# A transformer block on one core: ScalarE takes the first fourteen attention units, and VectorE the residual

## The chip, the core and the metric

The kernel is one program on one NeuronCore of a Trainium2 chip. The metric is device time in microseconds (us), from the host's view of one execution; the profile shows one such execution, taken by the hardware profiler, and its span from the first instruction to the last. Engines are named as in the profile: PE is TensorE (matmul; PEld its weight loads), DVE is VectorE, ACT is ScalarE, POOL is GpSimd, SP is SyncE, which only issues DMAs here.

## What is computed

Input x is 8 sequences of 1024 tokens, 128 channels wide. With xn the layer norm of x, the block gives x + attention(xn) + experts(xn):

```python
x = L0_attn_x
xn = _layernorm(x, axis=-1)
x = x + _L0_attn_ref(xn, ...) + _L0_ffn_ref(xn, ...)
# attention: 8 heads, q and k two wide, v sixteen wide; leaky instead of plain scores
scores = jnp.einsum('bmhd,bnhd->bhmn', q, k) / math.sqrt(dqk)
scores = jnp.where(scores >= 0, scores, 0.2 * scores)
beta = jax.nn.softmax(scores, axis=-1)
out = jnp.einsum('bhmn,bnhd->bmhd', beta, v).reshape(B, M, C)
return gamma * out + x
# experts: RMS norm, softmax router over 16 experts, top 2, capacity 1024 rows an expert
pos = jnp.sum(jnp.cumsum(oh, axis=0) * oh, axis=-1) - 1
keep = pos < CAP
...
h = jax.nn.gelu(jnp.einsum('ech,efh->ecf', dm, fc1_weight) + fc1_bias[:, None, :], approximate=False)
out_mlp = jnp.einsum('ecf,ehf->ech', h, fc2_weight) + fc2_bias[:, None, :]
```

Twelve of the sixteen experts are MLPs; one gives zero, one copies, two give constants. Attention returns its own input too, so the residual is x + xn + gamma * attention + experts.

## The kernel before

Tokens lie in 64 tiles of 128 (partitions) x 128 channels: `y` holds x and becomes the output, `xn` the layer norm. The program has these stages.

**Projections** (`groups(prologue)` in every engine): 16 groups of four tiles. A helper runs 22 steps; at step n each engine does the parts of group n, n-1, n-2, ... whose turn it is, so that engines overlap by lags. TensorE transposes and multiplies (L780 q and k, L784 v and router, L801 directions, L774 the scores' bounds), ScalarE copies out of PSUM, VectorE splits and keeps maxima (L984, L988), GpSimd makes remainders (L410, L415), SyncE stores q and k parts to DRAM (`store_parts`). `groups` takes a table `meanwhile`: functions that an engine calls behind given steps.

**Routing** sits behind and inside the last steps. VectorE finds the two best experts (`first_value` ... `second_choice`, lines 1027 to 1048), counts them (L1067), scans (L1072); TensorE turns counts into positions with two matmuls (L809), VectorE reads these from PSUM (L1076, L1080, semaphore `at_rdy`). GpSimd makes indices and weights (lines 590 to 610). ScalarE meanwhile makes the residual in place, `y = (1 + rstd) * y - mean * rstd`, 64 activations at L702. The scratch of the routing lies in `pr`, the buffer that attention's exponentials also use; the exponentials' first buffers are free early, the seventh unit waits for `route`.

**Attention of three sequences** (`attention(0, BH)`), then **twelve experts**, then **attention of the other five**. Attention goes by units: a pass is one sequence, four heads and 512 queries and has 16 units, 64 units a sequence. For unit i, TensorE makes scores into a PSUM ring of three slots (L820, semaphore `s1`), VectorE rectifies them in place (L1112, `relu`), TensorE adds the linear part and the shift (L830, `s2`), ScalarE takes the exponential (L724, `exps`), and TensorE multiplies with the values (L850, `pv`). Behind a pass VectorE transposes the sums (L1088), GpSimd divides (`quotient`, L445), SyncE moves them across partitions (`spread`, L334, 16 DMAs), GpSimd adds them to `y` (L458).

**Scatter.** During the first attention GpSimd sends the rows of xn to their expert slots in DRAM (`disp`) with 128 indirect DMAs (L496), eleven or twelve a pass for eleven passes; it also scales xn by `r2` (L491), a sequence at a time. `paced` makes a scatter wait for a number of exponentials. The quotient of pass p-1 stands in the middle of the scatters of pass p, in GpSimd's program order.

**Experts.** SyncE's queue holds, in this order: the spread of pass 9, a wait for all scatters (`scat`), the loads of expert 0 (weights and rows of `disp`), the spread of pass 10, a wait, the loads of expert 1; then, in a loop, the store of an expert and the loads of the one after next. VectorE's `turn_rows(e)` scales the weights (L1130) and transposes the rows (L1133), `expert_rows(e)` adds the second bias (L1142); TensorE runs L890 and L901, ScalarE the Gelu. GpSimd has a loop of its own beside them: for each of 8 batches of eight tiles eight instructions of 128x1024 (L623, L631, L634, L637) add the copy and constant experts and a bias to `y`, reading `xn`, which they overwrite.

Most waits are written out by hand as semaphore counts: `wait_ge(S["s1"], i + 1)`. An engine runs its program strictly in order, so what stands behind a wait waits too.

Of the kernel before, what the change touches and what calls it, by code (L numbers as in the profile page):

```python
# [12 lines left out]
P = 128  # L13
# [47 lines left out]
TURN = 5  # L61
BLOCK = 32
# [39 lines left out]
def build(nc, x, consts, w_qk, b_qk, w_vr, b_v, r_b, n_w, n_w_row, w1t, b1, w2t, b2, cvec, gamma, out):  # L102
# [4 lines left out]
    with ExitStack() as ctx:  # L107
# [3 lines left out]
        def sem(name):  # L111
# [23 lines left out]
        (mean, var, rstd, r2, s4, s5, s6, s7) = (st[:, k, :] for k in range(8))  # L135
        y_scale, y_bias = s6, s4
# [19 lines left out]
        moved = sb("moved", [P, 2, HG, GT, DV])  # L156
        rowones = sb("rowones", [1, M], BF16)
# [15 lines left out]
        rt = [ef[:, k, :] for k in range(2 * HG)]  # L173
        ex = rt[1]
        rbf = [rt[k // 2].bitcast(BF16)[:, (k % 2) * NT * E:(k % 2 + 1) * NT * E] for k in range(4 * HG)]
        oh1, oh2, rank_of, reset, cnt, incl = rbf[4:10]
        prod = rt[5], rt[6]
        small = rt[7].rearrange("p (k t) -> p k t", t=NT)
# [6 lines left out]
        xt = sb("xt", [P, CAP])  # L185
# [11 lines left out]
        ps_acc = ps[:, 6:8, :]  # L197
# [5 lines left out]
                 "qz_init weighted at_rdy sum_rdy inv_rdy row_step route ones_rdy max_rdy off_rdy reset_rdy r_exp cnt_rdy pos_rdy ztile init_rdy kz_init "  # L203
                 "ld0 ld1 vp_rdy s1 relu s2 exps pv acc_evac o_rdy turned rg_rdy att_rdy spread0 spread1 y_att "
# [33 lines left out]
        CO0 = 2  # L238

# [20 lines left out]
        def _(sp):  # L260
# [35 lines left out]
            groups(store_parts)  # L296
            for u in range(2):
                sp.wait_ge(S[f"parts_out{u}"], 64 * B)
                sp.wait_ge(S[f"shift_out{u}"], 16 * B)
            sp.wait_ge(S["kz_init"], 16 * NHG * HG)  # L300

            def load_operands(b, hg):
# [3 lines left out]
                for g in range(HG):  # L306
# [8 lines left out]
                    sp.dma_start(q2[o:o + 1, hg, :], qrows[NPROD:NROW, :]).then_inc(S[f"ld{hg}"], 16)  # L315

# [27 lines left out]
            for hg in range(NHG):  # L344
                load_operands(0, hg)
# [50 lines left out]
        def _(pool):  # L396
# [23 lines left out]
            pool.wait_ge(S["zero_in"], 16 * E_MLP)  # L420
# [132 lines left out]
            def attention(b0, b1, move):  # L553
                first, last = b0 * NPB, b1 * NPB - 1
                for p in range(first, last + 1):
                    b = p // NPB

                    def results():

                        if p % NPB == 0:  # L560
                            value_rows(b, 1)
# [16 lines left out]
            value_rows(0, 0)  # L578
# [33 lines left out]
            pool.sem_inc(S["route"], 1)  # L612
            pool.wait_ge(S["y_upd"], B)
# [31 lines left out]
        def _(act):  # L645
# [9 lines left out]
            act.activation(r2, s5, ACT.Sqrt).then_inc(S["stat_a"], 1)  # L655
# [37 lines left out]

            def expert_exponentials():
# [12 lines left out]
            expert_exponentials()  # L707
            for b in range(B - 3, B):
                residual(b)
            act.wait_ge(S["at_rdy"], 1)  # L710
# [7 lines left out]
            def exponentials(i):  # L718
# [5 lines left out]
                act.activation(pr[:, c % BUFS, 2 * pair:2 * pair + 2, :], ring[i % RING], ACT.Exp, scale=SLOPE  # L724
                               ).then_inc(S["exps"], 1)

            def attention(b0, b1):
                first, end = b0 * NUB, b1 * NUB
                for i in range(first, end):
                    if i == (BUFS - 1) * PAIRS + 1:  # L730
                        act.wait_ge(S["route"], 1)
# [481 lines left out]
```

## Time and profile before

| what | us |
|---|---|
| median of 3 runs | 930.86 (929.11 to 931.17) |
| the profiled execution | 931.08 |
| its span | 929.3 |

| engine | busy us | share of the span | instructions |
|---|---|---|---|
| PE | 851.2 | 92% | 7403 |
| DVE | 763.9 | 82% | 883 |
| ACT | 676.9 | 73% | 787 |
| POOL | 602.1 | 65% | 610 |

Of the span, the projections end at about 97 us, the routing at about 126, the first attention at about 362, the experts at about 533. The shares are averages over stages with different limits, so they are read stage by stage: in the routing TensorE hardly works, in attention VectorE and TensorE are both near full, in the experts TensorE alone is.

In a row of the timeline stand the start, the length, engine and line, the operation, what it writes and reads with partitions x elements, how many instructions are merged, and in brackets the idle time of the engine before it and what ended that. SPq is SyncE's DMA queue. "issue" is time in which an engine waited for nothing that the profile shows.

### The profile page before, as it was taken

The numbers are of one execution on the slowest core, as the hardware profiler recorded it, in microseconds if no ns is written. First come the engines' busy times: TensorE is split into PE (matmuls) and PEld (weight loads), VectorE is DVE, ScalarE is ACT, GpSimd is POOL, SyncE is SP. The second block draws the span as 40 slices with busy tenths as digits, with TensorE's granted clock in tenths as the row PEclk, the third lists the DMA queues.
The fourth block names the chain that finished last, engine by engine and source line by source line (L and its number), as shares of the span: only waits on it lengthen the run. The fifth ranks groups of instructions, "written<-read, shape, count | busy, mean of one in ns | idle before, by whom it ended". The sixth has DMA issues, their size and how long they took to land.

```text
span 929.3 us, 19960 instructions
## 1 busy us (share of the span) xinstructions
PE 851.2 (92%) x7403; PEld 338.5 (36%) x7404; DVE 763.9 (82%) x883; ACT 676.9 (73%) x787; POOL 602.1 (65%) x610
## 2 busy tenths in 40 slices
PE   0687269999999999999999999999999999999997
PEld 0454112222222224776776722222222222222222
DVE  5798899999999996322321399999999999999996
ACT  0578888888888888344344388888888888888886
POOL 3355247777777662999999426567566675766772
PEclk9999669999999999999999999999999999999999
DMA  8733101111111014355364111012112011200202
GB/s 220 301 68 77 31 28 33 49 40 52 50 25 37 21 30 92 88 137 126 86 141 125 40 48 40 21 28 59 29 30 60 25 35 27 77 23 17 68 16 54
DMA packets 130167, 59.34 MB, mean 64 GB/s; under 512 B 83498, under 2 KB 120194, under 8 KB 130080
## 3 DMA queue, kind: packets, MB, share of 16 engines
q1 hardware_dynamic: 120464, 48.06, 20.3%
q0 software_dynamic: 8192, 9.37, 3.7%
q8 instruction: 54, 0.88, 0.4%
q10 hardware_dynamic: 1424, 0.76, 0.4%
q14 instruction: 33, 0.27, 0.1%
HBM read 31.58 MB, written 30.02 MB: 66 GB/s over the span
## 4 chain that ended last, share of the span: by engine, by line
PE 59%; DVE 25%; issue 8%; ACT 3%; POOL 2%; DMA 1%; SPq 1%; POOLq 0%; DVEq 0%; ACTq 0%
DVE ps L1112 20%; PE ps L850 18%; PE ps L830 11%; PE ps L820 11%; PE ps L901 9%; PE ps L890 9%; DVE ot L1088 2%; PE ps L780 1%; DMA y<-in_x 1%; ACT pr L675 1%; DVE bst L947 1%; ACT pr L724 1%; SPq L262 1%; POOL ot L410 1%; ACT va L684 1%
## 5 line engine op out<-in xcount | busy, mean ns | idle before, releaser
L1112 DVE TENSOR_SCALAR ps<-ps 128x1024 f32<-128x1024 f32 x512 | 600.3, 1224 | 15.1 <-PE ps L820 12.1
L724 ACT ACTIVATE pr<-ps 128x1024 f32<-128x1024 f32 x512 | 524.0, 1024 | 104.6 <-PE ps L830 70.7
L850 PE MATMUL ps<-pr,vp 128*32 128x256 f32 x4096 | 327.7, 392 | 0.3
L830 PE MATMUL ps<-q,kz 64*128 64x512 bf16 x1024 | 200.6, 389 | 10.1 <-DVE ps L1112 4.3
L820 PE MATMUL ps<-q,kz 62*128 62x512 bf16 x1024 | 200.8, 390 | 2.9 <-DMA q<-parts_dram 1.4
L511 POOL DMA_INDIRECT xs<-eout,idxs x128 | 129.1, 1008 | 107.5 <-ACT pr L724 82.3
L496 POOL DMA_INDIRECT disp<-xn,idx x128 | 125.8, 983 | 50.4 <-issue 28.2
L745 ACT ACTIVATE pr<-ps,b1s 128x512 f32<-128x512 f32 x96 | 66.0, 687 | 96.4 <-PE ps L890 96.4
L830 PEld LDWEIGHTS ps<-q,kz 64*128 64x128 bf16 x1024 | 48.9, 92 | 226.1 <-DVE ps L1112 187.7
L850 PEld LDWEIGHTS ps<-pr,vp 128*32 128x32 f32 x4096 | 81.1, 108 | 120.5 <-issue 118.1
L1130 DVE TENSOR_SCALAR w<-w,nw 128x512 f32<-128x512 f32 x12 | 14.1, 1175 | 94.6 <-DMA pr<-disp 50.6
L901 PEld LDWEIGHTS ps<-w,pr 128*128 128x128 f32 x768 | 87.7, 192 | 6.2 <-issue 6.2
L820 PEld LDWEIGHTS ps<-q,kz 62*128 62x128 bf16 x1024 | 49.4, 93 | 106.9 <-ACT pr L724 76.7
L901 PE MATMUL ps<-w,pr 128*128 128x128 f32 x768 | 88.0, 275 | 0.0
L890 PE MATMUL ps<-xt,w 128*128 128x512 f32 x192 | 84.7, 593 | 0.6 <-issue 0.6
L634 POOL TENSOR_TENSOR y<-y,xn x24 | 56.6, 2358 | 4.9 <-POOL xn L631 4.9
L531 POOL TENSOR_TENSOR y<-y,xs 128x256 f32<-128x256 f32 x64 | 46.5, 727 | 11.4 <-POOL y L531 5.7
L458 POOL TENSOR_TENSOR y<-y,moved 128x256 f32<-128x256 f32 x32 | 23.3, 730 | 44.3 <-DMA moved<-att 28.5
L890 PEld LDWEIGHTS ps<-xt,w 128*128 128x128 f32 x192 | 35.5, 190 | 40.9 <-issue 40.9
L410 POOL TENSOR_TENSOR ot<-pr,parts 112x512 f32<-112x512 f32 x16 | 18.9, 1179 | 37.3 <-ACT parts L680 37.2
L524 POOL TENSOR_TENSOR xs<-xs,co 128x256 f32<-128x256 f32 x64 | 37.9, 616 | 0.6
L792 PE MATMUL ps<-cst,xn 128*128 128x128 f32 x64 | 10.5, 291 | 27.5 <-DVE xn L966 27.5
(120 smaller groups left out, 527.4 us busy)
## 6 DMA issues: line engine op xcount, KB each, us to landing
moved<-att SPq DMA_DIRECT2D x480, 8.0 KB
disp<-pr SPq DMA_DIRECT2D x12, 512.0 KB, 4.8
eout<-pr SPq DMA_DIRECT2D x12, 512.0 KB, 3.0
y<-in_x SPq DMA_DIRECT2D x8, 512.0 KB, 7.5
out<-y SPq DMA_DIRECT2D x7, 512.0 KB, 3.4
w<-in_w1t SPq DMA_DIRECT2D x12, 256.0 KB, 3.1
w<-in_w2t SPq DMA_DIRECT2D x12, 256.0 KB, 3.3
xs<-disp SPq DMA_DIRECT2D x24, 128.0 KB, 3.5
```

The source lines that it names most:

```text
L496: pool.indirect_dma_start(out=disp, out_offset=bass.IndirectOffsetOnAxis(ap=idx[:, k, s * TB + t:s * TB + t + 1], axis=0), in_=xn[:, s * T ...
L511: pool.indirect_dma_start(out=g1[:, g % 2, t, c, :], out_offset=None, in_=eout, in_offset=bass.IndirectOffsetOnAxis(ap=idxs[:, c, GB * i + ...
L531: pool.tensor_tensor(yt, yt, rows[:, :, c, :], ALU.add).then_inc(S["comb" if c else "weighted"], 1)
L634: pool.tensor_tensor(yb, yb, xb, ALU.add).then_inc(S["pool_step"], 1)
L724: act.activation(pr[:, c % BUFS, 2 * pair:2 * pair + 2, :], ring[i % RING], ACT.Exp, scale=SLOPE).then_inc(S["exps"], 1)
L745: act.activation(hs[:, f, half * HALF:(half + 1) * HALF], ps[:, 2 + n % 4, :], ACT.Gelu, bias=b1s[:, u, f:f + 1]).then_inc(S["gel"], 1)
L820: last = pe.matmul(ring[i % RING][:, k, :], kz[r:r + ONES, hg, pair, kc * P:(kc + 1) * P], q2[r:r + ONES, hg, qh * HALF:(qh + 1) * HALF], ...
L830: last = pe.matmul(ring[i % RING][:, k, :], kz[r:r + TILE, hg, pair, kc * P:(kc + 1) * P], q2[r:r + TILE, hg, qh * HALF:(qh + 1) * HALF], ...
L850: last = pe.matmul(acc[p % 2][32 * g:32 * g + 32, cols], vp[:, hg, kc, g, :], pr[:, c % BUFS, g % PAIRS * 2 + g // PAIRS, cols], start=(kc ...
L890: pe.matmul(ps[:, 2 + n % 4, :], w1[:, 2 * u * FFN + f * P:2 * u * FFN + (f + 1) * P], xt[:, half * HALF:(half + 1) * HALF], start=True, s ...
L901: mm = pe.matmul(o, hs[:, f, j * P:(j + 1) * P], w1[:, (2 * u + 1) * FFN + f * P:(2 * u + 1) * FFN + (f + 1) * P], start=(f == 0), stop=(f ...
L1112: dve.tensor_scalar(s, s, 0.0, 1.0 / SLOPE - 1.0, ALU.max, ALU.mult).then_inc(S["relu"], 1)
```

## The change

- ScalarE does the first fourteen units alone, while VectorE is still in the routing: it rectifies them (a Relu in place, `relu_a`) and takes their exponentials, in a written-out order behind the last steps of the projections. These units use two slots of the PSUM ring (banks 0 to 3), and the position matmuls move from banks 6 and 7 to banks 4 and 5. TensorE's order is written out likewise: `first_scores`, `second_pair`, `third_pair`, `later_pairs`; the position matmuls stand between the units. VectorE starts with unit 14.
- The table of the exponential is loaded behind step 3 of the projections (`ready(ACT.Exp)`).
- SyncE loads the operands of the first sequence between the stores of the projections, one head behind each of the steps 8 to 15, and not behind all of them.
- The residual leaves ScalarE. VectorE makes it in the experts as `y = y + xn * rms`, 64 instructions (`scalar_tensor_tensor`): eight ahead of expert 1, 32 behind `expert_rows(0)`, 24 behind `expert_rows(1)`. GpSimd's loop waits for `y_upd`, batch by batch; the first attention's sums are then already in `y`. The wait of GpSimd for the whole residual ahead of attention goes, and so does ScalarE's wait for `route`.
- The routing's scratch moves from `pr` to buffers that are free then (`w1`, `xs`, `parts`, `ot`, `xt`). GpSimd copies both halves of the first values ahead of the routing.

```diff
+FIRST = 14
...
-        (mean, var, rstd, r2, s4, s5, s6, s7) = (st[:, k, :] for k in range(8))
-        y_scale, y_bias = s6, s4
+        (mean, var, rstd, r2, s4, s5, s6, rms) = (st[:, k, :] for k in range(8))
...
+        flat = [w1[:, k * NT * E:(k + 1) * NT * E] for k in range(2)]
+        xflat = xs[:].rearrange("p u t c -> p (u t c)")
+        ex = flat[0]
+        oh1, oh2, rank_of, cnt, reset, incl = (
+            half.bitcast(BF16) for v in (flat[1], xflat, pflat) for half in (v[:, 0:NT * E // 2], v[:, NT * E // 2:NT * E]))
+        prod = flat[0], ot[:].rearrange("p a m -> p (a m)")
+        small = xt[:].rearrange("p (k t) -> p k t", t=NT)
...
-        ps_acc = ps[:, 6:8, :]
+        ps_pos = ps[:, 4:6, :]
...
+        def slot(i):
+
+            return ring[i % 2 if i < FIRST else i % RING]
...
+            def first_operands(k):
+
+                if k == 0:
+                    sp.wait_ge(S["kz_init"], 16 * NHG * HG)
+                    for u in range(2):
+                        sp.wait_ge(S[f"parts_out{u}"], 64)
+                        sp.wait_ge(S[f"shift_out{u}"], 16)
+                load_operands(0, k // HG, range(k % HG, k % HG + 1))
+
+            groups(store_parts, {8 + k: lambda k=k: first_operands(k) for k in range(H)})
...
-            pool.wait_ge(S["zero_in"], 16 * E_MLP)
+            pool.wait_ge(S["dir_rdy"], 2 * B)
+            for u in range(2):
+                pool.wait_ge(S[f"parts_out{u}"], 64 * B)
...
-            value_rows(0, 0)
+            for hg in range(NHG):
+                value_rows(0, hg)
...
-            pool.sem_inc(S["route"], 1)
-            pool.wait_ge(S["y_upd"], B)
             attention(0, BH, scatter)
...
                 pool.wait_ge(S["scat"], 16 * GS)
+                pool.wait_ge(S["y_upd"], b + 1)
...
-            def residual(b):
-
-                for t in range(b * TB, (b + 1) * TB):
-                    last = act.activation(y[:, t, :], y[:, t, :], ACT.Identity, scale=y_scale[:, t:t + 1],
-                                          bias=y_bias[:, t:t + 1])
-                last.then_inc(S["y_upd"], 1)
-
-            groups(prologue, {2 * B + 1 + b: lambda b=b: residual(b) for b in range(B - 3)})
...
+            def rectify(i):
+
+                act.wait_ge(S["s1"], i + 1)
+                act.activation(slot(i), slot(i), ACT.Relu, scale=1.0 / SLOPE - 1.0).then_inc(S["relu_a"], 1)
...
+            groups(prologue, {
+                3: lambda: ready(ACT.Exp),
+                2 * B + 1: lambda: first_units(("R", 0), ("R", 1), ("E", 0), ("E", 1), ("R", 2)),
+                2 * B + 2: lambda: first_units(("R", 3), ("E", 2), ("E", 3), ("R", 4), ("R", 5)),
+                2 * B + 3: lambda: first_units(("E", 4), ("E", 5), ("R", 6), ("R", 7)),
+                2 * B + 5: lambda: first_units(("E", 6), ("E", 7), ("R", 8), ("R", 9))})
+            expert_exponentials()
+            for i in range(8, FIRST, PAIRS):
+                first_units(("E", i), ("E", i + 1))
+                if i + PAIRS < FIRST:
+                    first_units(("R", i + 2), ("R", i + 3))
+            attention(0, BH, FIRST)
...
+            def first_pair(j, behind):
+
+                shifted(2 * j)
+                if j > 0:
+                    values(j - 1, 0)
+                behind()
+                shifted(2 * j + 1)
+                if j > 0:
+                    values(j - 1, 1)
...
+            def first_scores():
+
+                pe.wait_ge(S["v_rdy"], 2 * B)
+                pe.wait_ge(S["xnt_rdy"], 2 * B)
+                scores(0)
+                pe.wait_ge(S["v_evac"], 2 * B)
+                pe.wait_ge(S["lg_rdy"], 2 * B)
+                scores(1)
+                first_pair(0, nothing)
+                scores(2)
...
+            def later_pairs():
+
+                scores(7)
+                for j in range(3, FIRST // 2 - 2):
+                    first_pair(j, nothing)
+                    scores(2 * j + 2)
+                    scores(2 * j + 3)
+                positions(0, cbf[:, C_TRI:C_TRI + P], cnt)
+                first_pair(FIRST // 2 - 2, lambda: positions(1, onesb[:], incl))
+                scores(FIRST - 2)
+                scores(FIRST - 1)
+                pe.wait_ge(S["pos_read"], 2)
+                first_pair(FIRST // 2 - 1, lambda: scores(FIRST))
+                scores(FIRST + 1)
+
+            groups(prologue, {2 * B: first_scores, 2 * B + 1: second_pair, 2 * B + 2: third_pair})
+            later_pairs()
+            attention(0, BH, FIRST)
...
+            def residual(first, last):
+
+                for b in range(first, last):
+                    for t in range(b * TB, (b + 1) * TB):
+                        ins = dve.scalar_tensor_tensor(out=y[:, t, :], in0=xn[:, t, :], scalar=rms[:, t:t + 1],
+                                                       in1=y[:, t, :], op0=ALU.mult, op1=ALU.add)
+                    ins.then_inc(S["y_upd"], 1)
+
+            dve.wait_ge(S["y_att"], BH * NPB)
+            residual(0, 1)
+            for u in range(2):
+                turn_rows(u + 1, 1 - u)
+                expert_rows(u, u)
+                residual(1 + 4 * u, 5 + 3 * u)
+            with dve.Fori(1, E_MLP // 2 - 1) as k:
```

## Rows read from the trace of the kernel before

**Rows 1.** The page's chain that ended last, by line, shares of the span.
```profile
DVE ps L1112 20%; PE ps L850 18%; PE ps L830 11%; PE ps L820 11%; PE ps L901 9%; PE ps L890 9%; DVE ot L1088 2%; PE ps L780 1%; DMA y<-in_x 1%; ACT pr L675 1%; DVE bst L947 1%; ACT pr L724 1%; SPq L262 1%; POOL ot L410 1%; ACT va L684 1%
```

**Rows 2.** The chain in order of time, 376:410 us; start, length, what.
```profile
377.22 0.59 issue
...
377.81 7.11 PE ps L890 x16
...
392.06 6.87 PE ps L890 x16
```

**Rows 3.** Timeline of VectorE, routing; start, length, line, operands, count [idle before].
```profile
123.64 2.35 DVE L1080 TENSOR_REDUCE pr<-pr 128x64 f32<-128x1024 f32 x2
...
125.90 3.59 DVE L1112 TENSOR_SCALAR ps<-ps 128x1024 f32<-128x1024 f32 x3
...
134.03 12.03 DVE L1112 TENSOR_SCALAR ps<-ps 128x1024 f32<-128x1024 f32 x10 [0.74 <-PE ps L820]
```

**Rows 4.** Timeline of ScalarE, routing.
```profile
98.27 3.19 ACT L702 ACTIVATE y<-y,st 128x128 f32<-128x128 f32 x8
...
117.15 1.28 ACT L697 ACT_TABLE_LOAD   x1
```

**Rows 5.** Timeline of TensorE, routing.
```profile
102.91 0.61 PE L774 MATMUL ps<-hat,bok 128*32 128x512 bf16 x1
```

**Rows 6.** Stretches: length, busy time (instructions) by engine, granted clock, DMA.
```profile
core 0: us, PE busy (x) PEld busy (x) DVE busy (x) ACT busy (x) POOL busy (x), PEclk, DMA share, GB/s
...
104.00:116.00 12.00, 0.71 (x2) 0.20 (x2) 11.66 (x16) 11.95 (x31) 0.00 (x0) 0.50 0.01 1
...
134.00:140.00 6.00, 5.92 (x64) 1.77 (x68) 5.84 (x5) 4.95 (x6) 4.53 (x9) 1.00 0.00 0
```

**Rows 7.** GpSimd: scatter grouped, 140:337 (count, busy, mean, idle before); its timeline.
```profile
L496 POOL DMA_INDIRECT disp<-xn,idx x122 | 119.8, 982 | 48.7 <-issue 26.5 <-ACT pr L724 20.9 <-POOL xn L491 1.0
...
140.52 1.23 POOL L496 DMA_INDIRECT disp<-xn,idx  x1 [1.15 <-issue]
...
337.01 0.63 POOL L445 TENSOR_TENSOR att<-ot,rg 128x256 f32<-128x256 f32 x1
```

**Rows 8.** Timeline of SyncE's queue at the start of the experts.
```profile
337.67 10.79 SPq L334 DMA_DIRECT2D moved<-att  x16
...
367.32 4.87 SPq L361 DMA_DIRECT2D pr<-disp  x4
```

**Rows 9.** Timeline of VectorE, experts 0 to 2.
```profile
374.15 2.41 DVE L1130 TENSOR_SCALAR w<-w,nw 128x512 f32<-128x512 f32 x1 [8.01 <-DMA pr<-disp]
...
377.64 1.18 DVE L1142 TENSOR_TENSOR pr<-ps,parts 128x1024 f32<-128x1024 f32 x1
...
387.47 1.02 DVE L1130 TENSOR_SCALAR w<-w,nw 128x512 f32<-128x512 f32 x1 [8.65 <-DMA xs<-disp]
...
388.41 1.23 DVE L1133 STREAM_TRANSPOSE xt<-xs 128x1024 f32<-128x1024 f32 x1
```

**Rows 10.** Timeline of GpSimd in its own loop beside the experts.
```profile
369.16 2.35 POOL L623 TENSOR_TENSOR xn<-xn,nwr 128x1024 f32 x1 [0.36 <-POOL co L618]
...
371.78 1.90 POOL L631 TENSOR_TENSOR xn<-xn,co  x1 [0.26 <-POOL xn L623]
...
385.85 2.35 POOL L637 TENSOR_TENSOR y<-y,bvg 128x1024 f32 x1 [0.19 <-POOL y L634]
...
388.16 2.55 POOL L623 TENSOR_TENSOR xn<-xn,nwr 128x1024 f32 x1
```

**Rows 11.** Timeline of VectorE and GpSimd in the projections, two groups.
```profile
48.31 1.11 DVE L966 TENSOR_SCALAR xn<-y,st 128x128 f32<-128x128 f32 x4
...
49.08 1.35 POOL L410 TENSOR_TENSOR ot<-pr,parts 112x512 f32<-112x512 f32 x1 [0.64 <-ACT parts L680]
...
50.11 0.41 DVE L1010 TENSOR_TENSOR lg<-lg,rb 128x64 f32<-128x64 f32 x1
...
97.51 0.22 DVE L1010 TENSOR_TENSOR lg<-lg,rb 128x64 f32<-128x64 f32 x1
```

**Rows 12.** The page's group of GpSimd's L410: busy, mean ns, idle before.
```profile
L410 POOL TENSOR_TENSOR ot<-pr,parts 112x512 f32<-112x512 f32 x16 | 18.9, 1179 | 37.3 <-ACT parts L680 37.2
```

More of the change, by code:

```diff
@@ L238, in build @@
         CO0 = 2
+        def slot(i):
+            return ring[i % 2 if i < FIRST else i % RING]
+        assert FIRST % RING == 2 and FIRST % 2 == 0
         def unit_of(i):
@@ L692, in prologue, with ready @@
                     act.copy(xnt[:, u, :], ps_t).then_inc(S["xnt_rdy"], 1)
+            def ready(function):
+                act.activation(table[:], gam[:], function, scale=0.0)
             def expert_exponentials():
@@ L723, in exponentials, with attention @@
                     wait_done(act, "pv", c - BUFS + 1)
-                act.activation(pr[:, c % BUFS, 2 * pair:2 * pair + 2, :], ring[i % RING], ACT.Exp, scale=SLOPE
+                act.activation(pr[:, c % BUFS, 2 * pair:2 * pair + 2, :], slot(i), ACT.Exp, scale=SLOPE
                                ).then_inc(S["exps"], 1)
-            def attention(b0, b1):
+            def attention(b0, b1, done=0):
                 first, end = b0 * NUB, b1 * NUB
-                for i in range(first, end):
-                    if i == (BUFS - 1) * PAIRS + 1:
-                        act.wait_ge(S["route"], 1)
+                for i in range(first + done, end):
                     if i == BH * NUB:
@@ L802, in prologue @@
                     last.then_inc(S["dir_rdy"], 1)
-            groups(prologue)
-            for n, (lhs, rhs) in enumerate(((cbf[:, C_TRI:C_TRI + P], cnt), (onesb[:], incl))):
-                pe.wait_ge(S["cnt_rdy"], n + 1)
-                for half in range(2):
-                    last = pe.matmul(ps_acc[:, half, :], lhs, rhs[:, half * HALF:(half + 1) * HALF], start=(n == 0),
-                                     stop=(n == 1))
-            last.then_inc(S["pos_rdy"], 1)
             def scores(i):
@@ L867, in ahead, with attention @@
                     scores(i)
-            def attention(b0, b1):
+            def attention(b0, b1, done=0):
                 first, end = b0 * NUB, b1 * NUB
-                for i in range(first, end):
+                for i in range(first + done, end):
                     shifted(i)
@@ L904, in expert, with positions, nothing, second_pair @@
                 mm.then_inc(S["fc2"], 1)
-            ahead(0, AHEAD)
-            attention(0, BH)
+            def positions(n, lhs, rhs):
+                pe.wait_ge(S["cnt_rdy"], n + 1)
+                for half in range(2):
+                    last = pe.matmul(ps_pos[:, half, :], lhs, rhs[:, half * HALF:(half + 1) * HALF], start=(n == 0),
+                                     stop=(n == 1))
+                if n == 1:
+                    last.then_inc(S["pos_rdy"], 1)
+            def first_pair(j, behind):
[6 more added lines that the diff above has]
+                    values(j - 1, 1)
+            def nothing():
+                pass
+            def first_scores():
[7 more added lines that the diff above has]
+                scores(2)
+            def second_pair():
+                scores(3)
+                first_pair(1, nothing)
+                scores(4)
+                scores(5)
+            def third_pair():
+                first_pair(2, nothing)
+                scores(6)
+            def later_pairs():
[14 more added lines that the diff above has]
+            attention(0, BH, FIRST)
             for u in range(2):
```

85 lines of the change are left out of this document (39 added, 46 removed).

## The prediction

> **What bounds the kernel now.** I read the chain of waits first. By line it is VectorE's rectifying pass (L1112), then TensorE's lines of attention and experts [rows 1]; so VectorE sets the pace in attention and TensorE in the experts. Its stretch at the expert start then shows where one begins to bind: TensorE stands 0.59 us before expert 1 at 377.81 and is gapless from there, expert 2 at 392.06 [rows 2]. Then I read the routing, engine by engine. VectorE ends the position sums at 123.64 + 2.35 = 125.99, begins unit 0 at 125.90 and is steady from 134.03, unit 6: ten units in 12.03 [rows 3]. ScalarE is free of the projections from 98.27 and spends the time on the residual [rows 4].
>
> GpSimd needs a look of its own. It gets the positions at 125.99, issues its first scatter at 140.52, 14.5 later, and comes to the ninth pass's quotient at 337.01 [rows 7]. SyncE stores that result from 337.67 and only behind it, in its queue, loads the experts' rows: those of expert 1 from 367.32, for 4.87 [rows 8]. VectorE idles 8.01 for just that load at 374.15 [rows 9]. So expert 1 does not hang on the end of attention; it hangs on GpSimd's scatter, 40.1 us behind 337.67.
>
> **Part by part: the first units.** Fourteen units taken off VectorE are 14 x 1.2 = 17 us [rows 3]. They need ScalarE twice each. A pass of ScalarE over 128x1024 is not in my rows; VectorE takes 1.2 for the same shape, an upper end, and I take 1.03 for ScalarE, so 28 passes are 29 us from 98.27, to about 130 with TensorE's answers between them. VectorE's own routing work keeps its length but now waits in three places. (1) The next to last hat (L988) waits for a small matmul (L774) that TensorE now issues behind the scores of units 0 to 2, so behind three ScalarE passes: 98.27 + 3.1 = 101.4, then a score and L774, near 102.2. Before, L774 had run long ago, and VectorE came there at about 100.7: 1.5 to 1.7. (2) The last hat waits for the L774 behind unit 5's scores. ScalarE does two more passes, then needs the matmuls behind hat (1), near 104 to 104.7, then four more passes: 108 to 108.8, with score and L774 near 108.6 to 109.6. VectorE is there six us behind (1), near 108: 0.5 to 1.7. (3) The second position matmul now stands in TensorE's queue behind ScalarE's first pass of unit 10: twelve passes and some small ones behind (2), near 123 to 123.8; its sums come at 124 to 126, VectorE's scan ends near 122 to 123.5, 1.1 of this gap was there before: 0.6 to 1.6. Low ends hold with TensorE at the higher of its two levels, high ends at the lower; it sits at 0.50 through 104 to 116 and L774 takes 0.61 there [rows 5, 6]. Sum 2.6 to 5.0; I take 3.7. Positions at 129.7, VectorE's unit 14 there and not at about 143.6 (134.03 + 8 x 1.2): attention ends 11 to 12 us sooner.
>
> GpSimd's scatter starts 3.7 later, though. From there it runs at its own pace more than before. Of 48.7 us of idle before its 122 issues, 122 x 0.30 and 8 x 0.67 (behind a scaling) come with each issue; 6.7 are waits [rows 7]. With attention 12 sooner and the scatter 3.7 later these go. Bounds 4 to 6.7, I take 5; a value copy moved ahead adds 0.5. The Exp table load moves from 117.15 into group 3 of the projections; it takes 1.28 [rows 4], and ScalarE's pause there covers part: 0 to 1.3, I take 0.7. The twelve load issues per half that SyncE now makes between its stores fall into its pauses; nothing. The arithmetic on the mean and two tiny VectorE ops that go: nothing. So expert 1's data come at -0.7 (that is 0.7 + 3.7 - 5.5, or -1.1), bounds -5 to +3; I take -1. **The 12 us of attention are thus mostly not kept**: they end as TensorE idling before the experts.
>
> **The residual.** ScalarE's residual [rows 4] was under the routing, on an engine with nothing better to do. Now VectorE does it in the experts: 64 tiles, eight ahead of expert 1's weights, 32 between the results of expert 0 and the weights of expert 2 (turn_rows(2)), 24 before those of expert 3. By length it fits: four 128x128 tiles took 1.11 [rows 11], 0.26 apart, so 32 are 8.3, and VectorE idled 8.65 before 387.47 [rows 9].
>
> But each tile reads two SBUF tensors (xn and y), and GpSimd is at that time in its own loop over SBUF, 1.90 to 2.55 long instructions with 0.26 or less between them, none at a batch's edge (385.85 + 2.35 = 388.20 against 388.16), 19.0 a batch [rows 10]. What happens to such an op is shown by one pair of rows. L1010 (lg + rb, both SBUF) takes 0.22 at 97.51. At 50.11 it meets GpSimd's L410, in flight from 49.08 to 50.43, and takes 0.41: it ends at 50.52, 0.09 behind GpSimd [rows 11]. It was held until GpSimd's instruction ended. L1130, another form, is held alike: at 374.15 it takes 2.41 under an instruction that ran to 376.3, at 387.47 only 1.02 [rows 9]. The Trainium skill, "SBUF — State Buffer", section "Who interferes with whom", states this for two SBUF inputs against a GpSimd instruction that reads SBUF: whichever started first keeps the shared port to its end. By the rule the tiles are held, and the sum is the 983 below; were the 0.41 a chance, it would be 930. The trace agrees with the rule, 0.41 against 0.22.
>
> So tiles pass only between GpSimd's instructions. The held tile finishes as the port comes free, the next starts some 0.07 later, ahead of GpSimd's next (0.26), and a third, 0.26 on, finds GpSimd waiting. I take two per pause, one at the edge: 15 per 19.0, 1.27 each. Bounds: one per pause (2.4) and three (0.86); not held is a rival.
>
> The sum: expert 0's results end at 377.64 + 1.18 = 378.8 [rows 9]. 32 x 1.27 = 40.5, to 419.3. Expert 2's weights and transpose took 387.47 to 388.41 + 1.23 = 389.64, for TensorE at 392.06 [rows 2, 9], so they could start by 389.9: late by 29.4. From that start: 2.2 for weights and transpose, 1.2 for results, 24 x 1.27 = 30.5, 2.2 again, 36.1; TensorE starts 2.2 in and has one expert of 14.2 (392.06 less 377.81) to live on: idle 19.7 more. Together 49.1. Behind each pause TensorE may start again at its lower level (1.2 of 2.4 GHz): in the routing the grant was 0.50, and from unit 0 at 125.90 to the full grant at 134 it worked some 8 us at half speed [rows 3, 6]. That costs up to 4 each, or nothing where the grant does not fall; I take 2, so 4. Later experts find their rows loaded and TensorE as before, and GpSimd's loop ends well before the last expert.
>
> The profiled execution ran 931.1 around its span of 929.3, 0.2 above the median of 930.86; 931.1 - 1 + 49.1 + 4 = 983.2, as a median 983.
>
> **The rivals.** (a) *One tile per pause*: GpSimd gets the port before the second tile. 8 tiles in 19.0: 76 and 57 us in place of 40.5 and 30.5, 62 more, about 1040. For it: no row shows two tiles in one pause. Against it: where L966's tiles ran to 49.42 beside L410 of 49.08, L410 took 1.35 and not its mean of 1.18 [rows 11, 12], so a ready VectorE op can go first. (b) *The tiles are not held*, L1010's 0.41 being chance: then 32 tiles take the 8.3 that VectorE had idle, nothing is late, and only the scatter decides: 931.1 - 1 = 930, with its bounds 926 to 934. One row speaks against it [rows 11]. The side changes here: at 0.26 a tile the cover of 8.65 + 2.4 is enough; from 0.35 a tile on expert 2 is late. (c) *Not held, and the scatter keeps up*: if expert 1 hung on the end of attention the whole 11 to 12 would stay, less 0.7: 920. Against it is the 8.01 wait for that load. (d) *Slower without the residual*: the three new waits at their high ends, the table load in full and no scatter wait saved give +3 to +5; it decides if positions come later than 131.5. It lies in (b)'s range.
>
> **How the numbers follow.** Held, two to three per pause: 0.56, 955 to 1000 by its own bounds (0.86 a tile gives about 26 + 4 - 1, so 960; the high end is the clock and a slower pause). (a) 0.13, (b) 0.25, (c) 0.06. Of (b) I give half to faster by over 0.2%, a third to the same, the rest to slower; 0.2% is about what a measurement of this kernel can tell from no change. Faster 0.18, same 0.08, slower 0.74. The range must reach over (b) and (c) to hold 8 in 10: 920 to 995; the likeliest case alone has 955 to 1000.
>
> **What would show it.** Right: the position sums near 129 to 131; unit 14 of L1112 right behind; attention's last unit near 348, TensorE then idle until near 361; expert 1 within 5 us of 377; then residual tiles with a mean far above 0.3 us, in pairs between GpSimd's instructions, and TensorE idle some 29 us before expert 2 and 20 before expert 3, released by VectorE's weights. Wrong: residual tiles of 0.3 us straight through GpSimd's instructions; then the time is (b)'s. If expert 1 starts near 366, the scatter did not bind.

## The result

The changed kernel takes 982.91 us (median of 4 runs, 982.17 to 985.58) against 931.01: a ratio of 1.056, 95% interval 1.0537 to 1.0582. The forecast was 983. The profiled execution took 985.58, its span is 983.8; that is 54.5 more than the span of before. It is the slowest of the four, 2.7 above their median, so the rows below add up to more than the 51.9 between the medians.

The chain of waits by line, on the page, has a new member, VectorE's residual L1234 (lines are those of the changed kernel; L1193 is the rectifying pass, L914 and L925 are the experts' matmuls):

```profile
DVE ps L1193 20%; PE ps L874 14%; PE ps L854 9%; PE ps L841 9%; DVE y L1234 7%; PE ps L914 6%; PE ps L925 6%; SPq L351 2%; DVE ot L1169 2%; POOL disp L513 2%; DMA y<-in_x 1%; SPq L376 1%; PE ps L810 1%; DVE bst L1032 1%; DMA pr<-disp 1%
```

Where the time went is seen in the timeline of TensorE, from the end of attention to expert 4 (each L914 with 16 matmuls begins an expert, 0 to 4; expert 0 in two pieces of 4 and 12):

```profile
348.58 2.28 PE L874 MATMUL ps<-pr,vp 128*32 128x256 f32 x32
360.89 3.75 PE L914 MATMUL ps<-xt,w 128*128 128x512 f32 x4 [10.03 <-issue]
...
378.98 7.10 PE L914 MATMUL ps<-xt,w 128*128 128x512 f32 x16 [1.04 <-issue]
...
422.53 9.38 PE L914 MATMUL ps<-xt,w 128*128 128x512 f32 x16 [29.30 <-DVE xt L1214]
...
456.39 9.52 PE L914 MATMUL ps<-xt,w 128*128 128x512 f32 x16 [17.34 <-DVE xt L1214]
...
472.89 7.03 PE L914 MATMUL ps<-xt,w 128*128 128x512 f32 x16
```

In before, attention's last matmuls and the starts of experts 2, 3 and 4 (L850 and L890 are there what L874 and L914 are here) are:

```profile
360.29 2.28 PE L850 MATMUL ps<-pr,vp 128*32 128x256 f32 x32
...
391.89 7.03 PE L890 MATMUL ps<-xt,w 128*128 128x512 f32 x16
...
405.91 7.03 PE L890 MATMUL ps<-xt,w 128*128 128x512 f32 x16
...
419.92 7.03 PE L890 MATMUL ps<-xt,w 128*128 128x512 f32 x16
```

Attention ends at 348.58 + 2.28 = 350.9, at 362.6 in before, and TensorE then stands 10.03 idle. Expert 1 begins at 378.98, not 377.81 [rows 2]. Expert 2 waits 29.30 and expert 3 17.34, both for VectorE's transpose. The same stretch on VectorE:

```profile
369.94 2.77 DVE L1234 SCALAR_TENSOR_TENSOR y<-xn,st,y 128x128 f32<-128x128 f32 x8 [3.23 <-POOL y L475]
375.81 1.91 DVE L1211 TENSOR_SCALAR w<-w,nw 128x512 f32<-128x512 f32 x1 [3.10 <-DMA pr<-disp]
...
379.91 39.19 DVE L1234 SCALAR_TENSOR_TENSOR y<-xn,st,y 128x128 f32<-128x128 f32 x32
419.01 2.12 DVE L1211 TENSOR_SCALAR w<-w,nw 128x512 f32<-128x512 f32 x1
421.05 1.23 DVE L1214 STREAM_TRANSPOSE xt<-xs 128x1024 f32<-128x1024 f32 x1
...
423.32 29.64 DVE L1234 SCALAR_TENSOR_TENSOR y<-xn,st,y 128x128 f32<-128x128 f32 x24
```

The first eight tiles run while GpSimd rests and take 2.77, the first of them held by a short GpSimd instruction; the 32 take 39.19 and the 24 take 29.64, 1.22 and 1.24 a tile. 29 of the 64 are held, that is, take 0.9 or more. All 64 tiles by duration (minimum, median, maximum in ns), and one pair of them beside the GpSimd instruction of that moment:

```profile
L1234 DVE SCALAR_TENSOR_TENSOR y<-xn,st,y x64: 325/340/2444, 369.9 to 452.6; 128x128 f32<-128x128 f32 x64
```
```profile
382.33 2.69 DVE L1234 SCALAR_TENSOR_TENSOR y<-xn,st,y 128x128 f32<-128x128 f32 x2
```
```profile
382.44 2.44 POOL L651 TENSOR_TENSOR y<-y,xn  x1 [0.18 <-POOL xn L648]
```

The pair starts at 382.33. Its first tile is the short kind (median 0.34); its second is caught by GpSimd's instruction of 382.44 and ends at 385.02, 0.14 behind GpSimd's 384.88. This is the two tiles per pause of the forecast.

The granted clock in the wait for expert 2, and at the start of experts 2 and 3, where it is the lower of the two levels (a row holds the start and end, the length, busy time of PE, PEld, DVE, ACT and POOL, then the granted clock and the DMA share and rate):

```profile
390.00:420.00 30.00, 3.22 (x29) 3.03 (x28) 30.00 (x24) 0.00 (x0) 27.64 (x13) 0.61 0.00 0
422.00:425.00 3.00, 2.47 (x3) 1.18 (x4) 3.00 (x5) 0.36 (x1) 2.74 (x2) 0.50 0.13 41
456.00:460.00 4.00, 3.61 (x5) 1.55 (x6) 1.26 (x2) 0.69 (x1) 3.55 (x3) 0.50 0.37 111
```

In the routing VectorE's rows are these (L1095 is the last of the logits, which end the projections, L1073 is the hat, L1157 the reading of the positions, L1161 their sums):

```profile
99.94 0.23 DVE L1095 TENSOR_TENSOR lg<-lg,rb 128x64 f32<-128x64 f32 x1
...
104.97 0.69 DVE L1073 SCALAR_TENSOR_TENSOR hat<-ps,hat 128x512 bf16<-128x512 f32 x1 [1.86 <-PE ps L804]
...
113.29 0.69 DVE L1073 SCALAR_TENSOR_TENSOR hat<-ps,hat 128x512 bf16<-128x512 f32 x1 [2.53 <-PE ps L804]
...
127.75 1.22 DVE L1157 TENSOR_TENSOR w<-ps,w 128x1024 f32<-128x1024 f32 x1 [0.70 <-PE ps L934]
...
131.28 1.21 DVE L1161 TENSOR_REDUCE xt<-ot 128x64 f32<-128x1024 f32 x1
```

and GpSimd's scatter, grouped over 146:339.5, its first instruction and the quotient of the ninth pass:

```profile
L513 POOL DMA_INDIRECT disp<-xn,idx x122 | 119.8, 982 | 44.8 <-issue 26.6 <-ACT pr L732 15.6 <-POOL xn L508 1.9
```
```profile
146.95 1.23 POOL L513 DMA_INDIRECT disp<-xn,idx  x1 [1.15 <-ACT pr L732]
...
338.87 0.63 POOL L462 TENSOR_TENSOR att<-ot,rg 128x256 f32<-128x256 f32 x1
```

### The profile page after: what moved, and what is told of

Its sections match the earlier page's. It is cut to its first block, busy times and chain, and to the rows that moved or that the text cites. A ratio compares the mean times of both kernels' runs of the same rounds, so it can differ in the third digit from the quotient of the medians.

```text
span 983.8 us, 19965 instructions
## 1 busy us (share of the span) xinstructions
PE 859.9 (87%) x7403; PEld 341.7 (35%) x7404; DVE 818.7 (83%) x931; ACT 663.5 (67%) x738; POOL 603.6 (61%) x610
## 4 chain that ended last, share of the span: by engine, by line
PE 45%; DVE 34%; issue 7%; SPq 5%; POOL 3%; DMA 2%; ACT 2%; POOLq 0%; DVEq 0%; ACTq 0%
DVE ps L1193 20%; PE ps L874 14%; PE ps L854 9%; PE ps L841 9%; DVE y L1234 7%; PE ps L914 6%; PE ps L925 6%; SPq L351 2%; DVE ot L1169 2%; POOL disp L513 2%; DMA y<-in_x 1%; SPq L376 1%; PE ps L810 1%; DVE bst L1032 1%; DMA pr<-disp 1%
## 5 line engine op out<-in xcount | busy, mean ns | idle before, releaser
L1193 DVE TENSOR_SCALAR ps<-ps 128x1024 f32<-128x1024 f32 x498 | 583.4, 1224 | 13.8 <-PE ps L841 11.0
L874 PE MATMUL ps<-pr,vp 128*32 128x256 f32 x4096 | 327.9, 393 | 1.1 <-POOL vp L450 0.8
L914 PE MATMUL ps<-xt,w 128*128 128x512 f32 x192 | 91.9, 633 | 58.3 <-DVE xt L1214 47.1
L874 PEld LDWEIGHTS ps<-pr,vp 128*32 128x32 f32 x4096 | 81.2, 108 | 121.5 <-issue 119.1
L925 PEld LDWEIGHTS ps<-w,pr 128*128 128x128 f32 x768 | 87.7, 192 | 6.2 <-issue 6.2
L925 PE MATMUL ps<-w,pr 128*128 128x128 f32 x768 | 88.0, 275 | 0.0
L1234 DVE SCALAR_TENSOR_TENSOR y<-xn,st,y 128x128 f32<-128x128 f32 x64 | 71.6, 1192 | 3.2 <-POOL y L475 3.2
L914 PEld LDWEIGHTS ps<-xt,w 128*128 128x128 f32 x192 | 38.0, 204 | 103.1 <-issue 102.9
L475 POOL TENSOR_TENSOR y<-y,moved 128x256 f32<-128x256 f32 x32 | 23.3, 730 | 44.8 <-DMA moved<-att 28.1
```

The source lines that it names most:

```text
L874: last = pe.matmul(acc[p % 2][32 * g:32 * g + 32, cols], vp[:, hg, kc, g, :], pr[:, c % BUFS, g % PAIRS * 2 + g // PAIRS, cols], start=(kc ...
L914: pe.matmul(ps[:, 2 + n % 4, :], w1[:, 2 * u * FFN + f * P:2 * u * FFN + (f + 1) * P], xt[:, half * HALF:(half + 1) * HALF], start=True, s ...
L925: mm = pe.matmul(o, hs[:, f, j * P:(j + 1) * P], w1[:, (2 * u + 1) * FFN + f * P:(2 * u + 1) * FFN + (f + 1) * P], start=(f == 0), stop=(f ...
L1193: dve.tensor_scalar(s, s, 0.0, 1.0 / SLOPE - 1.0, ALU.max, ALU.mult).then_inc(S["relu"], 1)
L1234: ins = dve.scalar_tensor_tensor(out=y[:, t, :], in0=xn[:, t, :], scalar=rms[:, t:t + 1], in1=y[:, t, :], op0=ALU.mult, op1=ALU.add)
```

## The experiments

The theory: the residual's tiles are held by GpSimd's instructions, that is the whole loss, and the 12 us of attention are lost because experts 0 and 1 hang on GpSimd's scatter. The kernel before was run beside each set: 931.52 us beside the first four experiments, 930.52 beside the next four, 930.76 beside the two mended kernels.

### The residual left out

```diff
-                pool.wait_ge(S["y_upd"], b + 1)
...
-            residual(0, 1)
...
-                residual(1 + 4 * u, 5 + 3 * u)
```

> The changed kernel without its 64 residual tiles (the output lacks the layer norm's term), and without GpSimd's wait for them; all else as in the changed kernel. Theory (the residual tiles are held by GpSimd's loop, and the first units bring nothing because expert 1 hangs on the scatter): expert 2 starts 14.2 us behind expert 1, near 393, expert 3 near 407, and the whole takes 930 to 935 us, likeliest 932. Rival 1 (the first units do bring their 11 to 12 us once the residual is gone): 920 to 922. Rival 2 (something other than the residual makes the 50 us): 960 or more.

Measured: 933.13 us (10 runs), ratio 1.0017 [1.0003, 1.0032] to before. Some 50 us go with the residual, and what stays is not faster than before but 1.6 us slower: both rivals fall. The first units' gain ends as TensorE's idle time ahead of expert 0 (timeline of TensorE):

```profile
362.88 3.38 PE L913 MATMUL ps<-xt,w 128*128 128x512 f32 x4 [9.46 <-issue]
...
380.95 7.10 PE L913 MATMUL ps<-xt,w 128*128 128x512 f32 x16 [1.95 <-issue]
```

### GpSimd's loop behind the residual

```diff
-                pool.wait_ge(S["y_upd"], b + 1)
...
+            pool.wait_ge(S["y_upd"], B)
             with pool.Fori(0, B) as b:
```

> The changed kernel with one edit: GpSimd waits for all of the residual ahead of its loop, not batch by batch; the computation is the whole one. Theory (VectorE's tiles are held by GpSimd's instructions): with GpSimd standing, a tile comes every 0.26 us, expert 2 starts near 393 and expert 3 near 407; GpSimd's loop runs from about 401 to about 553, so that its gather starts some 15 us later than before; 932 if that is hidden, up to 947 if not. Rival (the tile is slow in itself, or held by TensorE, ScalarE or the loads): tiles at 1.2 us as in the changed kernel, 983 or more.

Measured: 931.13 us (8 runs), ratio 0.9999 [0.9986, 1.0013]. The same 64 instructions, with GpSimd standing (by duration, the longest being the first, beside a short instruction of GpSimd; then the timeline):

```profile
L1234 DVE SCALAR_TENSOR_TENSOR y<-xn,st,y x64: 341/346/935, 370.2 to 399.8; 128x128 f32<-128x128 f32 x64
```
```profile
379.74 8.48 DVE L1234 SCALAR_TENSOR_TENSOR y<-xn,st,y 128x128 f32<-128x128 f32 x32
390.91 0.49 DVE L1211 TENSOR_SCALAR w<-w,nw 128x512 f32<-128x512 f32 x1 [2.69 <-DMA xs<-disp]
```

32 tiles take 8.48, 0.26 apart, and VectorE is idle again ahead of the weights of expert 2. One moved wait gives back the whole loss. The median is even 2.0 below that of the kernel without a residual. One difference is in the traces: there GpSimd's loop runs and the scaling of expert 1's weights takes 2.03 (at 377.67), here 0.49 (at 376.32); that this makes the 2.0 is not shown. GpSimd pays: its loop starts at 400.56 and the gather behind it at 552.98, 15.5 later than before (537.45),

```profile
400.56 2.35 POOL L640 TENSOR_TENSOR xn<-xn,nwr 128x1024 f32 x1 [29.58 <-DVE y L1234]
```
```profile
552.98 0.20 POOL L480 COPY idxs<-idx 128x16 int32<-128x16 int32 x1
```

and none of it shows in the time.

### One operand out of PSUM

```diff
-                                                       in1=y[:, t, :], op0=ALU.mult, op1=ALU.add)
+                                                       in1=ps[:, 0, 0:C], op0=ALU.mult, op1=ALU.add)
```

> The changed kernel with one operand of the residual tile moved: in1 is read from an idle PSUM bank and not from y (so what is added is not y; the output is not the reference's); the instruction, its count, its length and its output in y are the same. Theory (held because both inputs come out of SBUF): tiles of 0.26 to 0.35 us straight through GpSimd's instructions, expert 2 near 393, 930 to 936 us. Rival (held for the write into y, or for anything that the edit leaves in place): 1.2 us a tile, 980 to 985.

Measured: 933.81 us (8 runs), ratio 1.0019 [1.0004, 1.0035]. GpSimd's loop runs beside the tiles as in the changed kernel, and no tile is held:

```profile
L1234 DVE SCALAR_TENSOR_TENSOR y<-xn,st,ps x64: 339/342/346, 370.7 to 400.5; 128x128 f32<-128x128 f32 x64
```

The output still goes to y in SBUF, so it is the second input out of SBUF that is held, not the write.

### One input out of SBUF, in another form

```diff
-                        ins = dve.scalar_tensor_tensor(out=y[:, t, :], in0=xn[:, t, :], scalar=rms[:, t:t + 1],
-                                                       in1=y[:, t, :], op0=ALU.mult, op1=ALU.add)
+                        ins = dve.tensor_scalar(y[:, t, :], xn[:, t, :], rms[:, t:t + 1], None, ALU.mult)
```

> The changed kernel with tensor_scalar in place of scalar_tensor_tensor: y = xn * rms, one input out of SBUF, output in SBUF (y is not added, so the output is not the reference's). Theory A (two inputs out of SBUF are what is held, one is not): 0.26 us a tile, 930 to 936. Theory B (this form is held too, as the weights' scaling L1211, one SBUF input, took 0.48 with GpSimd idle and 2.11 beside its loop): tiles near 1.2 us, 975 to 985. The row of L1211 speaks for B.

Measured: 971.31 us (2 runs), a little below theory B's 975 and far from A's 936: this form is held with one input.

```profile
L1234 DVE TENSOR_SCALAR y<-xn,st x64: 261/276/2426, 370.5 to 439.9; 128x128 f32<-128x128 f32 x64
```

It costs less than the changed kernel because these tiles follow each other 0.2 apart (380.08, 380.28, 380.48), so that two or three pass in a pause where the other form has two: 24 of the 64 are held, against 29. The two forms together are what the Trainium skill, "SBUF — State Buffer", section "Who interferes with whom", says: two inputs out of SBUF contend with GpSimd's reads, and tensor_scalar may enter a mode that takes the shared port pair although it has one input. The runs agree with both.

### The residual alone, without the first units

```diff
-            groups(prologue, {2 * B + 1 + b: lambda b=b: residual(b) for b in range(B - 3)})
+            groups(prologue)
...
+            residual(0, 1)
+            for u in range(2):
+                turn_rows(u + 1, 1 - u)
+                expert_rows(u, u)
+                residual(1 + 4 * u, 5 + 3 * u)
```

> The kernel before with the residual alone moved: ScalarE's 64 activations in the routing go, VectorE makes it in the experts at the places of the change, GpSimd's loop waits batch by batch; no first units. Theory (the whole loss is the residual's and has nothing to do with the first units): expert 2 some 29 us late, expert 3 some 50, 980 to 986 us. Rival (it needs the first units too, which shift GpSimd's loop against the tiles): under 960.

Measured: 982.91 us (2 runs), the same median as the whole change. Its waits on TensorE:

```profile
422.94 9.72 PE L881 MATMUL ps<-xt,w 128*128 128x512 f32 x16 [31.71 <-DVE xt L1121]
...
458.85 8.84 PE L881 MATMUL ps<-xt,w 128*128 128x512 f32 x16 [19.04 <-DVE xt L1121]
```

The loss needs nothing of the first units.

### GpSimd's scalings left out

```diff
-                        pool.tensor_tensor(rows, rows, r2[:, s * TB:(s + 1) * TB].unsqueeze(2).broadcast_to([P, TB, C]),
-                                           ALU.mult).then_inc(S["scaled"], 1)
-                        pool.wait_ge(S["scaled"], s + 1)
```

> The changed kernel without its residual and without GpSimd's eight scalings of xn ahead of the scatter (the output lacks the layer norm's term, and the experts get rows that are not scaled). Theory (expert 0 and 1 hang on GpSimd's scatter and what SyncE has queued behind it): the scatter ends some 20 us sooner, the experts start when attention ends, expert 0 near 352 to 354 and not 361 to 363, without TensorE's pause, expert 1 near 366 to 368; 918 to 923 us, so that the first units' gain shows. Rival (attention's end or something else in the first units holds the experts): 931 to 934.

Measured: 922.42 us (4 runs), ratio 0.9903 [0.9881, 0.9925]; against 933.13 without this edit, 10.7 less, or 9.7 with each taken against the kernel before of its own set. The last scatter comes at 331.7 and not at 347.4, 15.7 sooner where some 20 were expected. Expert 0 follows attention without a pause, and its first four matmuls take 1.98 and not 3.38 to 3.75:

```profile
350.33 2.28 PE L870 MATMUL ps<-pr,vp 128*32 128x256 f32 x32
352.55 1.98 PE L910 MATMUL ps<-xt,w 128*128 128x512 f32 x4
```
```profile
325.11 10.61 SPq L351 DMA_DIRECT2D moved<-att  x16
```

SyncE's spread stands at 325.11, at 339.53 in the changed kernel. GpSimd's scatter is shown as what holds the experts.

### TensorE's order in the routing

```diff
                 scores(1)
+                for u in range(2):
+                    bounds(B - 2, u, 2 * B - 4 + u)
                 first_pair(0, nothing)
...
                     first_pair(j, nothing)
+                    if j == FIRST // 2 - 3:
+                        positions(0, cbf[:, C_TRI:C_TRI + P], cnt)
+                        positions(1, onesb[:], incl)
```

(`bounds` is the matmul that the hats wait for; the old places of these matmuls go.)

> The changed kernel without its residual (the output lacks the layer norm's term), TensorE's order changed: the two matmuls of steps 17 and 18 that VectorE's last two hats wait for are issued ahead of unit 0's shift, and both position matmuls ahead of the scores of units 10 and 11. Theory (the routing is late by the three waits behind ScalarE's passes, 1.9, 2.5 and 0.7 us in the changed kernel's trace): the two hat waits go, positions near 128.5 to 129.5 in place of 132.5 to 133.8, first scatter near 143, expert 0 some 4 us sooner, 928 to 930 us. Rival (the attention's own pace or the loads bind expert 0): 932 to 934.

Measured: 931.54 us (10 runs), against 933.13 without it. Both hat waits are gone, positions end at 128.50 + 1.21 = 129.7 (133.8 without the edit), first scatter at 144.18, expert 0 at 358.64 (timelines of VectorE and TensorE):

```profile
104.02 0.69 DVE L1079 SCALAR_TENSOR_TENSOR hat<-ps,hat 128x512 bf16<-128x512 f32 x1
...
109.97 0.68 DVE L1079 SCALAR_TENSOR_TENSOR hat<-ps,hat 128x512 bf16<-128x512 f32 x1
...
128.50 1.21 DVE L1167 TENSOR_REDUCE xt<-ot 128x64 f32<-128x1024 f32 x1
```
```profile
358.64 3.75 PE L916 MATMUL ps<-xt,w 128*128 128x512 f32 x4 [8.73 <-issue]
```

The mechanism is as expected, 4.2 us at expert 0 by the profiles; the medians moved by 1.6, less than the 3 to 5 expected, and by 0.6 with each taken against the kernel before of its own set. That is not clear of noise: the ratio to before is 1.0000 [0.9977, 1.0022], against 1.0017 [1.0003, 1.0032] without the edit. Part of the difference lies in the choice of the execution: the profiled one of the kernel without a residual was 935.36, 2.2 above its median, and this one 932.05, 0.5 above.

### The table of the exponential loaded late

```diff
-                3: lambda: ready(ACT.Exp),
...
-                2 * B + 1: lambda: first_units(("R", 0), ...
+                2 * B + 1: lambda: ready(ACT.Exp) or first_units(("R", 0), ...
```

> The changed kernel without its residual (the output lacks the layer norm's term), and with the table of the exponential loaded behind step 17, ahead of unit 0's rectifying, not behind step 3. Theory (the projections end 2.4 to 3.5 us later than before because the load in group 3 shifts ScalarE against the other engines for good): VectorE's last logits near 97.5 to 98.3 and not 99.7 to 100.8, positions 1.5 to 3 sooner, first scatter and expert 0 likewise, 930 to 932 us against 933. Rival (the operand loads in SyncE's queue do it): logits stay near 100, time 933 or, with the load in the path, 934.

Measured: 935.2 us (5 runs), ratio 1.004 [1.0016, 1.0065], not faster. The last logits (L1093) come at 100.23, 0.8 sooner than the 101.06 of the kernel without a residual but no sooner than the changed kernel's 99.94; the first hat waits 3.25 in place of 1.86. As the whole account my theory falls. Timelines of VectorE and, from the same kernel, of ScalarE and TensorE, with the granted clock of that stretch:

```profile
100.23 0.23 DVE L1093 TENSOR_TENSOR lg<-lg,rb 128x64 f32<-128x64 f32 x1
...
106.65 0.69 DVE L1071 SCALAR_TENSOR_TENSOR hat<-ps,hat 128x512 bf16<-128x512 f32 x1 [3.25 <-PE ps L802]
```
```profile
53.63 0.62 ACT L696 CAST parts<-pr 112x512 bf16<-112x512 f32 x1 [1.23 <-DMA parts_dram<-parts]
```
```profile
69.31 2.05 PE L808 MATMUL ps<-pr,wqk 128*112 128x512 f32 x2
```
```profile
69.00:71.50 2.50, 2.50 (x5) 1.14 (x5) 2.43 (x9) 0.65 (x2) 1.15 (x1) 0.50 0.02 5
```

Up to group 5 this kernel is only 0.2 behind before; then ScalarE waits 1.23 for a store of SyncE to land, and at the seventh logits the kernel is 1.3 behind. The changed kernel has the same wait, 1.38 long and ending at 54.69, 20 us ahead of its first operand load (74.69), so the operand loads aren't its cause either. Why that store lands later is open. At the tenth logits 0.9 more is lost, and here the changed kernel loses nothing: two projection matmuls that take 1.11 in the groups beside it take 2.05 at a granted clock of 0.50, the lower level, after 65 to 69, in which TensorE worked 2.2 of 4 us. So this run doesn't show the late table's worth by its last logits: it was spared the load's delay at group 4 and paid about as much to the clock.

### Two mended kernels

Both compute the whole. The first is GpSimd's late loop and TensorE's order together; the second has VectorE scale two sequences as well:

```diff
+SCALED = 2
...
+                        if s >= SCALED:
+                            pool.tensor_tensor(rows, rows, r2[...
...
+            for s in range(SCALED):
+                for t in range(s * TB, (s + 1) * TB):
+                    last = dve.tensor_scalar(xn[:, t, :], xn[:, t, :], r2[:, t:t + 1], None, ALU.mult)
+                last.then_inc(S["scaled"], 1)
```

> The whole computation: the changed kernel with GpSimd waiting for all of the residual ahead of its loop, and TensorE's order in the routing changed as in hats_first (the two matmuls for the hats ahead of unit 0's shift, both position matmuls ahead of the scores of units 10 and 11). Theory (the held tiles are the whole loss, the routing's waits cost what hats_first gave back): tiles 0.26 us apart, expert 0 near 358 to 359, 929 to 931.5 us, not to be told from before. Rival (GpSimd's later loop costs the gather more when the experts are earlier): 933 or more.

> As mended, and VectorE scales the first two sequences of xn (16 tiles of 128x128) behind the position sums, so that GpSimd scales six in place of eight on its way through the scatter. Theory (experts 0 and 1 hang on GpSimd's scatter; attention's end has 8 us to spare): first scatter 2 us sooner, scatter's end 5 us sooner, attention's end 4 to 5 us later, near 354 to 355, expert 0 near 354 to 356, 925.5 to 928.5 us. Rival (the scatter is paced by attention, not by GpSimd): scatter's end no sooner, 930 to 935.

Measured: 928.76 us (12 runs), ratio 0.998 [0.9964, 0.9995], just below the 929 to 931.5 expected, and 924.23 us (6 runs), ratio 0.9935 [0.9915, 0.9956], below the 925.5 to 928.5 expected. In the second, VectorE's 16 tiles take 3.97 and TensorE's pause before expert 0 is down to 2.06, after which it starts at the higher clock (granted 1.00 from 355 to 357):

```profile
129.65 3.97 DVE L1175 TENSOR_SCALAR xn<-xn,st 128x128 f32<-128x128 f32 x16
```
```profile
354.94 1.96 PE L919 MATMUL ps<-xt,w 128*128 128x512 f32 x4 [2.06 <-issue]
```

So a kernel with the first units comes out 6.5 us below before, once the residual keeps out of GpSimd's way and work is taken from the scatter's chain. How much of the 6.5 the first units bring is not shown: no run takes the scaling off GpSimd in the kernel before.

## Why the prediction was right, point by point

**The residual.** Held to the end of GpSimd's instruction, two tiles a pause, one at a batch's edge: as forecast, 1.22 to 1.24 a tile against 1.27. The pause ahead of expert 2 was forecast as 29.4 and is 29.30. That ahead of expert 3 was forecast as 19.7 and is 17.34; expert 2 itself took 2.35 longer at the lower clock (9.38, where a first pass takes 7.03), and 17.34 + 2.35 = 19.7. That both meet to 0.1 is in part luck: the 32 and the 24 tiles took 1.3 and 0.9 less than forecast, and weights and transpose behind them 3.3 each (419.01 to 421.05 + 1.23) where I took 2.2, as the scaling of the weights is held too. The two runs that change only GpSimd's wait and only the operand show the cause; L1010's one long duration [rows 11] pointed the right way, and rivals (a) and (b) fall.

**The clock.** I added 2 us for each pause. The two first passes lost 2.35 and 2.49, but the first of these fell into the time in which TensorE would have waited for VectorE anyway. It paid once, not twice. That the 4 us came out as a sum is luck: between expert 4 and the end of the span the lag grew by another 1.5, from 53.0 to 54.5, for which I had no term. Of it 0.48 is one wait of TensorE, ahead of expert 5 for VectorE's transpose; the rest is spread over many small gaps, and I have not found what makes them. In the kernels with the first units experts follow each other about 14.2 apart, in before and in the one with the residual alone 14.0; this is open. One thing goes with it in all twelve traces: the load of an expert's second weights takes 1.09 in SyncE's queue in the former and 0.56 in the latter, from expert 2 on. That it is the cause is not shown.

**The scatter.** Experts 0 and 1 hang on it, as forecast; without the scalings they don't, and the run comes out at 922, near rival (c)'s 920. But expert 1's data were to come at -1 and came at +1.7 (VectorE's 375.81 against 374.15). (My line for this has -0.7 for terms that add up to -1.1.) The step that failed is the lateness of the positions: 4.4 forecast, 3.7 for the waits and 0.7 for the table load, which my 129.7 left out; 6.5 measured (131.28 + 1.21 = 132.49 against 125.99), a little beyond the two high ends together (5.0 and 1.3). The waits' sum was near, by luck: 1.86 and 2.53 with 0.43 less at the third make 4.0, but each of the three lies outside its own bounds (1.5 to 1.7, 0.5 to 1.7, 0.6 to 1.6). What was mis-sized is the end of the projections, 0.7 forecast and 2.4 measured (the last logits, 99.94 against 97.51 [rows 11]). I had put it on the table load alone. The logits of the fourth group, in before and in the changed kernel:

```profile
46.64 0.23 DVE L1010 TENSOR_TENSOR lg<-lg,rb 128x64 f32<-128x64 f32 x1
```
```profile
48.03 0.23 DVE L1095 TENSOR_TENSOR lg<-lg,rb 128x64 f32<-128x64 f32 x1
```

The changed kernel is 0.4 behind at the third (42.83 against 42.41), 1.4 at the fourth, across the load, 2.4 at the seventh (61.40 against 59.04), and stays there. So the load's 0.7 measured 1.0, and a step of 1.0 at this group stands in every kernel with the load there and not in that with the late table. The 1.0 of groups 5 to 7, in which ScalarE's wait for the store falls, I had put at nothing; the 0.4 at the start differs from run to run (1.0 in the kernel without a residual, -0.5 in the one with the residual alone). The other term, what GpSimd makes up, was forecast at 5.5 and is 4.6: first scatter 6.43 late, quotient 338.87 against 337.01, 1.86 late; 3.9 of it is less idle time before the scatters (44.8 against 48.7 [rows 7]).

**Rival (d)**, slower by the first units alone, was to decide if positions came later than 131.5. They came at 132.5 to 133.8, and the kernel without its residual is 1.6 us slower than before, the one with the PSUM operand 2.3: there it was right in sign, below its 3 to 5 in size. With GpSimd's loop behind the residual, positions at 133.2, the time is that of before. So my forecast for the first units, 1 us faster, isn't borne out: they cost 0 to 2. The 50 us of the residual covered it.

**The sum.** By TensorE's starts the span of 54.5 more is: expert 1 late 1.2, expert 2 another 29.5, expert 3 19.8, its slow first pass 2.5, the rest 1.5. Forecast: -1, 29.4, 19.7, 4, which is 52.1. Against this execution the sum is 2.4 short, nearly all of it expert 1's; that the median of 982.91 falls on the 983 is luck to that extent, as the profiled execution lay 2.7 above it.

## What to carry to other kernels

Before work is given to an idle VectorE, look at what GpSimd runs in that stretch: a short VectorE instruction with two SBUF inputs (or a tensor_scalar with one) beside a gapless GpSimd loop is priced by GpSimd's pauses, not by its own length; one operand in PSUM, or a wait that lets the short work go first, takes the price away. A gain on an engine is only kept if the next stage hangs on that engine: here attention ended 12 us sooner, but the next stage hung on GpSimd, and the experts began sooner only once work was taken off GpSimd. Two losses behind the same late event don't add: the slow clock behind the pause ahead of expert 2 was hidden by the wait ahead of expert 3.

## What the hardware did that I had not expected

- tensor_scalar with one SBUF input of float32, 128x128, was held just as long as the form with two (maximum 2.43 against 2.44); a PSUM input freed the other form wholly (339 to 346 ns over 64).
- A pause of TensorE of 9 to 10 us ahead of expert 0 left the next four matmuls at 3.4 to 3.75 us, one of 2.06 at 1.96: the granted clock is 0.50 from 361 to 365 in the changed kernel, the lower of the two levels, and 1.00 from 355 to 357 in the mended one, the higher.
- GpSimd's loop may start 28 us later (400.56 against 372.93 in the changed kernel) and its gather 15.5 later than before without a measurable cost.
